# A four-block gated cross-attention model on one core: an older order of the lists in the first attention, four instead of eight products with zeros a batch, and exponentials read straight from PSUM in the fourth block

## The reference, cut to what matters

```python
x = x + jnp.tanh(g_xattn[0]) * _L0_xattn_ref(_layernorm(x, axis=-1), ctx_512, ...)   # 16 heads of 8
...
x = x + jnp.tanh(g_xattn[2]) * _L2_xattn_ref(_layernorm(x, axis=-1), ctx_512, ctx_512, ...)   # 16 heads of 8, biases
...
x = x + jnp.tanh(g_xattn[3]) * _L3_xattn_ref(_layernorm(x, axis=-1), ctx_512, ...)
# inside _L3_xattn_ref, _mha is called first on (x, x), 16 heads of 32, with a causal factor after the softmax:
a = jax.nn.softmax(jnp.einsum('bhsd,bhtd->bhst', q, k) * D ** (-0.5), axis=-1)
if causal:
    a = a * mask          # mask keeps t > s
o = jnp.einsum('bhst,bhtd->bhsd', a, v)
```

## Time and profile before

| | us |
|---|---|
| median of 3 runs | 5575.47 |
| lowest and highest | 5569.66, 5575.83 |
| the profiled execution | 5589.97 |
| its span | 5588.1 |
| busy over the span: PE, DVE, ACT, POOL | 4842.0, 3953.4, 2700.3, 2176.0 |
| first and last weighing in l0x | 49 and 531 |
| the same in l2x | 2296 and 2785 |
| l3a | about 3295 to 4207 |

### The profile page before, as it was taken

One profiled execution on the slowest core, in us unless ns is written; L12 is line 12 of the kernel. 1 busy time (PEld: TensorE's weight loads), 2 busy tenths in 40 slices (PEclk: granted clock), 3 DMA queues, 4 the chain that ended last, 5 costly groups with the idle time before them and its releaser, 6 DMA issues. The chain is left out here.

```text
span 5588.1 us, 132733 instructions
## 1 busy us (share of the span) xinstructions
PE 4842.0 (87%) x41659; PEld 3572.6 (64%) x41659; DVE 3953.4 (71%) x9897; ACT 2700.3 (48%) x5454; POOL 2176.0 (39%) x3095
## 2 busy tenths in 40 slices
PE   7888998999952799688889989889898899998898
PEld 4555667888852466455566667767776677776554
DVE  5666876777766333677767768989886789897544
ACT  4545774555530233454555545555553455554344
POOL 5443001100027100776533357777776433333200
PEclk9989999999975899899999999999998999999878
DMA  1002400000011333100100000000000000000000
GB/s 40 8 7 66 209 0 6 5 5 5 5 56 44 114 135 133 35 23 22 30 2 0 0 6 0 0 0 0 0 0 7 3 2 2 2 2 7 0 14 17
DMA packets 109012, 141.38 MB, mean 25 GB/s; under 512 B 35832, under 2 KB 83256, under 8 KB 103996
## 3 DMA queue, kind: packets, MB, share of 16 engines
q1 hardware_dynamic: 100544, 120.88, 6.3%
q0 software_dynamic: 8192, 16.79, 1.0%
HBM read 47.44 MB, written 58.72 MB: 19 GB/s over the span
## 5 line engine op out<-in xcount | busy, mean ns | idle before, releaser
L2213 POOL TENSOR_TENSOR l3a_probs<-l3a_probs,l3a_later 128x512 f32<-128x512 f32 x256 | 320.6, 1280 | 4.9 <-DVE l3a_total L2401 4.9
L2199 POOL TENSOR_TENSOR l3a_keys<-l3a_kT,head 128x2048 f32<-128x2048 f32 x64 | 230.4, 3600 | 232.2 <-ACT l3a_kT L2326 232.2
L181 POOL TENSOR_TENSOR l1x_ve<-l1x_mv,eps 128x1 f32<-128x1 f32 x64 | 12.2, 190 | 646.7 <-DVE l1x_mv L173 646.7
L2261 PE MATMUL l3a_scores<-l3a_keys,l3a_qT 128*128 128x512 f32 x512 | 255.5, 601 | 4.2 <-POOL l3a_keys L2199 4.2
L1696 POOL TENSOR_TENSOR l2f_hid<-l2f_prod,l2f_route 128x512 f32<-128x512 f32 x128 | 152.1, 1193 | 254.7 <-DVE l2f_prod L1843 251.3
L309 PE MATMUL l3a_po<-l3a_vals,l3a_probsT 128*128 128x32 f32 x2048 | 251.0, 271 | 0.1
L309 PEld LDWEIGHTS l3a_po<-l3a_vals,l3a_probsT 128*128 128x128 f32 x2048 | 250.2, 194 | 0.4 <-ACT l3a_probsT L290 0.4
L265 ACT ACTIVATE l3a_probs<-l3a_probs 128x512 f32<-128x512 f32 x256 | 161.7, 632 | 180.7 <-DVE l3a_probs L256 175.7
L1582 PE MATMUL l1e_h<-l1e_xhi,l1f_parts 128*128 128x512 f16 x640 | 205.1, 382 | 9.7 <-DVE l1e_gated L1640 8.2
L2199 POOL TENSOR_TENSOR l3c_keys<-l3c_kT,head 128x1232 f32<-128x1232 f32 x64 | 144.0, 2250 | 156.7 <-ACT l3c_kT L2326 156.7
L295 DVE SCALAR_TENSOR_TENSOR l1x_loT<-l1x_turned,l1x_hiT 77x512 f16<-77x512 f32 x256 | 168.9, 679 | 48.9 <-ACT l1x_hiT L288 48.9
(11 more groups left out here) (581 smaller groups left out, 17155.9 us busy)
## 6 DMA issues: line engine op xcount, KB each, us to landing
l_rows<-l0f_zeros SPq DMA_DIRECT2D x34, 1024.0 KB, 27.1
l1f_parts<-l1f_split SPq DMA_DIRECT2D x40, 512.0 KB, 3.6
l1e_x_in<-l_rows SPq DMA_DIRECT2D x40, 256.0 KB, 2.8
l1f_down<-l1f_w SPq DMA_DIRECT2D x40, 256.0 KB, 2.4
l_rows<-l1e_y_out SPq DMA_DIRECT2D x40, 256.0 KB, 2.7
l1f_w<-in_L_W SPq DMA_DIRECT2D x16, 256.0 KB, 3.6
out_x<-x_res SPq DMA_DIRECT2D x16, 256.0 KB, 2.0
x_res<-in_x SPq DMA_DIRECT2D x1, 3840.0 KB, 12.3
```

The costliest lines, as they stand in the source:

```text
L2199: pool.tensor_tensor(keys[it.par][:, :, :, :], kT[it.par][:, :, :].unsqueeze(2).to_broadcast([P, J, G4, T]), g.head32[:, :].unsqueeze(1).u ...
L2213: pool.tensor_tensor(v, v, later[:, :].unsqueeze(1).to_broadcast([P, 4, T]), ALU.mult).then_inc(s_masked, 1)
L2261: pe.matmul(scores[c][:, 0:G4 * T], qT[it.par][:, c, :], keys[it.par][:, c, :, :].rearrange("p h t -> p (h t)"), start=True, stop=True).th ...
```

## The change

Three edits. In l0x (`routed` false) each engine's list takes an older order; l2x keeps the present one. The condition for a product with zeros becomes one on every second piece, so four a batch in both stages. In l3a the queries are scaled by minus the scale as they are copied, VectorE takes the minimum over a bank instead of the maximum, the shift goes, and ScalarE takes the exponential of each head out of PSUM with the minimum as bias and a scale of -1; score waits for the exponential instead of the shift.

```diff
-                        if u < 2:
+                        if c < 8 and c % 2 == 0:
                             pe.matmul(po[:, HEADS * E1:BANK], blank[:, 0:P], blank[:, HEADS * E1:BANK], start=False, stop=False,
...
+    def exponential_of_bank(self, act, it, c):
+        a, b = self.first[c], self.first[c + 1]
+        act.wait_ge(self.s_max, nth(it, self.nb, c))
+        if (due := nth(it, self.nc_, ago=2)) is not None:
+            act.wait_ge(self.s_turn, due)
+        for h in range(a, b):
+            last = act.activation(self.probs[it.par][:, h, :], self.view(c)[:, h - a, :], ACT.Exp,
+                                  bias=self.mx[it.par][:, h:h + 1], scale=-1.0)
+        last.then_inc(self.s_exp, 1)
...
-                        pe.wait_ge(sm.s_shift, due)
+                        pe.wait_ge(sm.s_exp if first else sm.s_shift, due)
...
+                        act.activation(dst, pa[:, :], ACT.Copy, scale=-scale).then_inc(s_qT, 1)
...
-                    names = ("hat stats3 maximum0 stats2 shift0 maximum1 add shift1 maximum2 maximum3 shift2 shift3 sum0 "
-                             "sum1 stats1 sum2 sum3 divide")
+                    names = "hat stats3 maximum0 stats2 maximum1 add sum0 maximum2 sum1 maximum3 stats1 sum2 sum3 divide"
```

The lists of l0x after the change (the minus lines are those that l0x has before; l2x keeps them), one slot a line:

```diff
 POOL
-                lags = {"s1": 2, "value0": 2, "s2": 2, "bias": 2, "value1": 2, "s3": 2, "deviation": 0, "rest": 1, "next": 1, "rows": -1}
-                order = ["maxA s1 value0 maxB s2 rows",
-                         "bias maxA maxB value1 rows s3",
-                         "maxA deviation maxB rest rows",
-                         "maxA maxB next rows"]
+                    lags = {"deviation": 0, "rest": 1, "next": 1, "value0": 1}
+                    order = ["maxA maxB s1",
+                             "bias maxA s2 maxB value1 s3",
+                             "maxA deviation maxB rest",
+                             "next maxA maxB value0"]
 PE
-                order = ["weigh2-2 scoreA shiftB-1 turn0-1 turn_o-2 v1 output-2 scoreB turn1-1 turn2-1 mtA weigh0-1 shiftA mtB weigh1-1",
-                         "weigh2-2 scoreA shiftB-1 turn0-1 turn_o-2 x output-2 scoreB turn1-1 turn2-1 q mtA weigh0-1 shiftA mtB weigh1-1",
-                         "weigh2-2 scoreA shiftB-1 turn0-1 turn_o-2 k output-2 scoreB turn1-1 turn2-1 mtA weigh0-1 shiftA mtB weigh1-1",
-                         "weigh2-2 scoreA shiftB-1 turn0-1 turn_o-2 output-2 scoreB v0 turn1-1 turn2-1 mtA weigh0-1 shiftA mtB weigh1-1"]
+                    order = ["shiftB-1 turn0-1 scoreA turn_o-2 v1 output-2 scoreB mtA turn1-1 turn2-1 shiftA weigh0-1 mtB x weigh1-1 weigh2-1",
+                             "shiftB-1 turn0-1 scoreA turn_o-2 q output-2 scoreB mtA turn1-1 turn2-1 shiftA weigh0-1 mtB weigh1-1 weigh2-1",
+                             "shiftB-1 turn0-1 scoreA turn_o-2 k output-2 scoreB mtA turn1-1 turn2-1 shiftA weigh0-1 mtB weigh1-1 weigh2-1",
+                             "shiftB-1 turn0-1 scoreA turn_o-2 v0 output-2 scoreB mtA turn1-1 turn2-1 shiftA weigh0-1 mtB weigh1-1 weigh2-1"]
 ACT
-                order = ["mB-1 expB-1 o-2 high0-1 v0 high1-1 high2-1 mA expA",
-                         "mB-1 v1 expB-1 o-2 high0-1 x high1-1 high2-1 c mA q expA",
-                         "mB-1 expB-1 o-2 high0-1 high1-1 high2-1 mA k expA",
-                         "mB-1 expB-1 o-2 high0-1 high1-1 high2-1 mA expA"]
+                    order = ["expB-1 high0-1 o-2 c mA high1-1 high2-1 expA mB x",
+                             "v1 expB-1 high0-1 o-2 q mA high1-1 high2-1 expA mB",
+                             "expB-1 high0-1 o-2 mA high1-1 high2-1 k expA mB",
+                             "expB-1 high0-1 o-2 mA high1-1 high2-1 expA v0 mB"]
 DVE
-                order = ["rest2-2 v0 row0-2 divide-2 maxA row1-2 add-2 rest0-1 maxB rest1-1",
-                         "rest2-2 row0-2 v1 divide-2 maxA row1-2 add-2 rest0-1 maxB rest1-1 stats",
-                         "rest2-2 row0-2 q divide-2 maxA row1-2 add-2 rest0-1 maxB rest1-1",
-                         "rest2-2 k row0-2 divide-2 maxA row1-2 add-2 rest0-1 maxB norm rest1-1"]
+                    order = ["divide-2 maxA rest0-1 add-2 maxB v1 rest1-1 rest2-1 stats",
+                             "divide-2 maxA rest0-1 add-2 maxB rest1-1 rest2-1 q",
+                             "divide-2 maxA rest0-1 add-2 maxB rest1-1 rest2-1 k",
+                             "divide-2 maxA rest0-1 add-2 maxB v0 rest1-1 rest2-1 norm"]
```

More of the change, by code:

```diff
@@ L213, with __init__ @@
 class Softmax:
-    def __init__(self, st, g, banks, heads_of_bank, keys, scale, ps_turn, split=False):
+    def __init__(self, st, g, banks, heads_of_bank, keys, scale, ps_turn, split=False, direct=False):
+        self.direct = direct
         self.g, self.banks, self.keys, self.scale = g, banks, keys, scale
@@ L876, in _ @@
                     steps[f"weigh{u}"] = lambda it, j, u=u: weigh(it, j, u)
-                lags = {"v1": 2, "x": 1, "q": 1, "k": 1, "v0": 1}
-                order = ["weigh2-2 scoreA shiftB-1 turn0-1 turn_o-2 v1 output-2 scoreB turn1-1 turn2-1 mtA weigh0-1 shiftA mtB weigh1-1",
[3 rows of a table removed]
+                if routed:
+                    lags = {"v1": 2, "x": 1, "q": 1, "k": 1, "v0": 1}
+                    order = ["weigh2-2 scoreA shiftB-1 turn0-1 turn_o-2 v1 output-2 scoreB turn1-1 turn2-1 mtA weigh0-1 shiftA mtB weigh1-1",
[3 rows of a table added]
+                else:
+                    lags = {"x": 1, "q": 1, "k": 1, "v0": 1}
+                    order = ["shiftB-1 turn0-1 scoreA turn_o-2 v1 output-2 scoreB mtA turn1-1 turn2-1 shiftA weigh0-1 mtB x weigh1-1 weigh2-1",
[3 rows of a table added]
                 skewed(pe, n, slots(steps, lags, order), 8 if routed else 6)
@@ L1069, in _ @@
                     steps["row0"], steps["row1"] = lambda it, j: combine(it, j, 0), lambda it, j: combine(it, j, 1)
-                lags = {"v0": 2, "v1": 2, "stats": 0, "q": 1, "k": 1, "norm": 0, "row0": -1, "row1": -1}
-                order = ["rest2-2 v0 row0-2 divide-2 maxA row1-2 add-2 rest0-1 maxB rest1-1",
[3 rows of a table removed]
+                if routed:
+                    lags = {"v0": 2, "v1": 2, "stats": 0, "q": 1, "k": 1, "norm": 0, "row0": -1, "row1": -1}
+                    order = ["rest2-2 v0 row0-2 divide-2 maxA row1-2 add-2 rest0-1 maxB rest1-1",
[3 rows of a table added]
+                else:
+                    lags = {"stats": 0, "norm": 0, "q": 1, "k": 1, "v0": 1}
+                    order = ["divide-2 maxA rest0-1 add-2 maxB v1 rest1-1 rest2-1 stats",
[3 rows of a table added]
                 skewed(dve, n, slots(steps, lags, order), 8 if routed else 6)
@@ L2157, in l3_attention @@
         pa, po = st.ps("pa"), st.ps("po")
-        sm = Softmax(st, g, scores, [4] * 4, T, scale, turned, split=not first)
+        sm = Softmax(st, g, scores, [4] * 4, T, scale, turned, split=not first, direct=first)
         n3 = Norm(st, g, "n3", P, P)
@@ L2319, in fetch_q @@
                         act.wait_ge(sm.s_scores, due)
-                    act.copy(qT[it.par][:, :, :].rearrange("p j t -> p (j t)"), pa[:, :]).then_inc(s_qT, 1)
+                    dst = qT[it.par][:, :, :].rearrange("p j t -> p (j t)")
+                    if first:
+                        act.activation(dst, pa[:, :], ACT.Copy, scale=-scale).then_inc(s_qT, 1)
+                    else:
+                        act.copy(dst, pa[:, :]).then_inc(s_qT, 1)
                 def fetch_k(it):
```

53 lines of the change are left out of this document (38 added, 15 removed), and 9 rows, old and new, of the table order.

## The result

The changed kernel takes 5510.85 us in the median (5484.82 to 5523.67), the kernel before 5575.65 on the same chip: a ratio of 0.9873 over the runs, 95% interval 0.9852 to 0.9895 (the two medians alone give 0.9884). By the medians that is 65 us faster; 130 were forecast. The profiled execution of after took 5523.67 us (span 5521.9), 66.3 less than that of before.

| stage | before, us | after, us | difference | forecast |
|---|---|---|---|---|
| l0x | 478.8 | 426.1 | -52.7 | -40 |
| l2x | 486.2 | 480.9 | -5.3 | -28 |
| l3a | 908.4 | 900.7 | -7.7 | -62 |

The account below looks back on a forecast made before the run. TensorE was taken to bound l0x and l2x (VectorE close behind in l2x), VectorE l3a. Terms of -28, -40 and -62 sum to -130 us, from a median of 5575.47 to 5445 us; range 5400 to 5535.

Parts of the forecast that it names:

- Part 2: l0x: older lists, with the zeros halved, take a batch from 7.01 to 6.36 us, -40 us in all.
- The stop at the back edge of the loop is met four times either way: l0x: TensorE's stop at the loop's back edge stays, costed at nothing, with 2 us left to either side.
- The order alone is worth nothing: l0x: the older lists' gaps cost 0.25 us a batch against 0.21 idle now, so no gain by themselves.
- Part 1: l2x: four fewer products with zeros save 0.45 us a batch over some 62 batches, -28 us.
- Rival C: l0x and l2x: fewer zeros make TensorE's clock fall; 37 falls eat the 130 us, more make it slower; chance 0.09.
- the sign that was given for it: l0x or l2x: clock at 0.5 away from the back edges would show the clock falling for lack of zeros.
- Part 3: l3a: exponentials straight from PSUM remove four VectorE shifts a batch; about -1.0 us a batch, -62 us.
- the walk: l3a: stepping through the new cycle took a batch from 14.55 to 13.5 us.
- the wait for qT: l3a: TensorE's wait of 1.49 us a batch for ScalarE's copy of qT was to go.
- the wait ahead of weigh3: l3a: a new TensorE wait of 0.5 us before the last weighing, until ScalarE finishes the last probabilities.
- rival A: l3a: ScalarE replaces VectorE as bound, short activations costing the 452 ns row; no gain there, total 5507 us; chance 0.13.
- the -53 us by it: l3a: estimate by the skill's fixed activation costs, a bank taking 1.27 us and the batch ending near 13.7 us.

Follow-up runs that it names:

- e1: Kernel before with only the products with zeros halved (four a batch in l0x and l2x), order and exponentials as before; ratio 0.9911 to the kernel before.
- e2: Kernel before with only the older lists in l0x, eight products with zeros and the shift kept; ratio 0.9926 to the kernel before.
- e10: Changed kernel with GpSimd's mask in l3a cut to 16 of 128 columns; ratio 0.9858 to the kernel before.
- e5: Changed kernel with the newer lists in l0x too, instead of the older ones; ratio 0.9788 to the kernel before.
- e12: Changed kernel with newer l0x lists and, in l3a, ScalarE's last probabilities copied ahead of exp3, then all products with zeros removed from l2x; 0.9839 of the kernel before.

## Why the prediction was half right

The time lies in the range, 24 us under its upper end, and the sign is right. The sum of -130 is twice what came, and the three terms missed in both directions.

**Part 2, l0x: the gain is right in size by two errors.** "The stop at the back edge of the loop is met four times either way. I cost it at nothing" is the step that failed. The stops were worth 42 us, more than the whole term, and they went. Against it the steady gain is 7.01 - 6.64 = 0.37 a batch, 23 us and not 40: four products with zeros fewer give 0.46 (e1: two slots of four give 0.6, the others 0.3) and not 0.62, and the older lists take 0.09 of that back. Bumps of 1 to 4 us in six single batches cost some 12 more: -42 - 23 + 12 = -53, measured -52.7. "The order alone is worth nothing" holds for the steady batches and fails for the stage: -39.7 alone (e2), +13 to +20 beside the halved zeros (e10 and after against e5). A part can't be costed as if the other weren't there.

**Part 1, l2x: the step was right, the clock took it back.** Undisturbed batches lost 0.39 to 0.50 us, and 0.45 was taken: -28 us. Three stops went too, which the sum didn't have: -29, with the half clock behind them. The stage should have gained 57 and gained 5. The 52 in between lie within the at most 84 us that 167 us at half clock cost. Rival C named this mechanism, but as an all-or-nothing case with 9 in 100; the sign that was given for it, half clock away from the back edges, is what after shows. What its reason against it said, that the busy share hardly falls, was no protection. As a term of the sum it would have brought the forecast near: the trace of before already showed one fall without a stop in this stage. By the rule that was cited with C from the Trainium skill, "TensorE: Matmul & The Clock Gate", Part 1, throttled as the default, more falls were to be expected; after agrees with nine in place of four, and e12 with fifteen.

**Part 3, l3a: the walk was right, for every second batch.** The short batch is 13.50 as walked; the wait for qT is gone; the wait ahead of weigh3 is 0.38 to 0.44, 0.5 was walked; exponentials take 398 ns, 365 was taken, and neither the 452 of rival A:

```profile
L275 ACT ACTIVATE l3a_probs<-l3a_scores,l3a_mx 128x128 f32<-128x128 f32 x1024 | 298.6, 398 | 43.4 <-DVE l3a_mx L249 42.6
```

The figure by the Trainium skill, "ScalarE: Activation LUTs", section "What ACT_TABLE_LOAD costs", 387, is nearer than mine, and the -53 us by it wouldn't have come either. The step that failed is the silent one that VectorE's instructions keep their lengths when they move. The walk gave maximum0 its old place behind score0, while the whole chain ahead of it lies within 0.2 us of GpSimd's mask. In before the product ran just ahead of the mask and the addition under it (292 and 1324 ns in the mean); a cycle shorter by 1 us moved the product behind the mask's start in every second batch, 0.96 each, 30 us. The other part is the clock: 14 falls of 3.4 us in place of one, 1.68 us each (15.19 - 13.51), 22 us. -62 + 30 + 22 = -10, measured -7.7. Rival A's number, 5507, lies next to the result, but by chance: ScalarE's activations weren't its cause.

## What to carry to other kernels

A fixed order that another engine runs beside has a phase, and a shorter cycle moves the phase: before an instruction with two operands in SBUF is costed by its old length, look at what GpSimd does within some tenths of a microsecond of it. Idle time of an engine under "issue" that comes with extra packets of the instruction queue is worth its full length to whatever edit removes it, so it belongs in the sum with both signs and not at zero. Where dummy work is cut, the clock rows of the same stage are a term of the sum, not a rival. And one profile of a stage is one draw: before stage times of two kernels are compared, see whether the same waits stand in both, and whether the kernel before takes the same time on both chips.

## What was not expected of the hardware

One product of 128x128 on VectorE takes 0.29 or 1.25 us, by 0.2 us of order against a GpSimd instruction. TensorE stopped 3.63 and 2.48 us within one weighing, by all signs for its own instructions, with 9 to 10 packets of 16 KB fetched in a pass; other lists with the same number of instructions have no stop and fetch nothing in the loop. In l3a the clock fell once with TensorE 90% busy (before) and 14 times with it 96% busy (after), so a fuller engine is no protection there; why is open. And the same code of l2x took 455 to 482 us in four profiled executions and 512 and 519 in two, in which VectorE waited until over 0.4 us behind the start of the last product of a weighing in 29 and 30 of 64 batches.
